# A four-layer image kernel on Trainium2: constant products in layer 2's last rows, hats sent in two lots, and the last group's norm and convolution at other steps

## What is computed

```python
x = x + _L0_conv_ref(_gn(x), ...)   # 1x1 convolutions and a mixture of radial bases
x = x + _L1_conv_ref(_gn(x), ...)   # state-space block
x = x + _L2_conv_ref(_gn(x), ...)   # attention, 8 heads over 256 pixels
x = x + _L3_conv_ref(_gn(x), ...)   # deformable 3x3 convolution
```

```python
offset = conv2d(x, off_w, off_b)
mask = jax.nn.sigmoid(conv2d(x, mask_w, mask_b))
samp = deform_sample(x, offset, mask)
out = jnp.einsum('bckhw,ock->bohw', samp, weight.reshape(O, C, K * K))
```

## Time and profile before

| | us |
|---|---|
| median of 3 runs (510.03 to 511.04) | 510.09 |
| the profiled execution's own time | 507.26 |
| its span | 505.4 |
| granted TensorE clock, mean over the span | 0.926 |
| TensorE busy (matmul) | 428.1 (85%) |
| VectorE busy | 346.9 (69%) |
| ScalarE busy | 280.1 (55%) |
| POOL busy | 133.4 (26%) |

### The profile page before, as it was taken

The page is one execution under the profiler, slowest core; times in us unless marked ns, Lnnn a source line. Parts: engine busy times, 40 slices in busy tenths (PEclk is TensorE's granted clock), DMA queues, the critical chain, the costliest instruction groups (busy, mean ns, idle before and its releaser), DMA issues.

```text
span 505.4 us, 9183 instructions
## 1 busy us (share of the span) xinstructions
PE 428.1 (85%) x3362; PEld 226.7 (45%) x3362; DVE 346.9 (69%) x672; ACT 280.1 (55%) x515; POOL 133.4 (26%) x171
## 2 busy tenths in 40 slices
PE   1525876899999998679998989998899999699997
PEld 0214755745555565513434434344355445255442
DVE  4538886423343556997998878978577768477785
ACT  1279974123135433605877778965486657376342
POOL 4330002100000001774544222232165245065000
PEclk9855998899999998756999999999799999999999
DMA  5400000630000000793320204407803923833500
GB/s 148 122 1 1 0 0 1 133 75 0 1 0 1 0 1 1 189 310 88 86 85 2 55 12 106 101 2 189 187 2 73 205 57 67 185 53 67 137 13 10
DMA packets 20170, 34.97 MB, mean 69 GB/s; under 512 B 4992, under 2 KB 16608, under 8 KB 18592
## 3 DMA queue, kind: packets, MB, share of 16 engines
q1 hardware_dynamic: 16880, 24.53, 20.6%
q0 software_dynamic: 1712, 7.01, 5.0%
q10 hardware_dynamic: 1536, 2.86, 2.2%
HBM read 16.78 MB, written 5.24 MB: 44 GB/s over the span
## 4 chain that ended last, share of the span: by engine, by line
PE 35%; DVE 8%; DMA 6%; POOL 5%; issue 3%; SPq 2%; ACT 2%; ACTq 1%; POOLq 0%; DVEq 0%
PE L_banks L1691 8%; PE L_banks L1593 6%; PE L_banks L1560 5%; PE L_banks L1667 4%; POOL L_parts L969 2%; PE L_banks L1631 2%; PE L_banks L1639 2%; DVE L_mx L1163 2%; DMA L_hats<-L_parts 2%; POOL L_rest L963 2%; DMA L_hat<-L_offsets 1%; SPq L1014 1%; ACTq L913 1%; PE L_banks L1573 1%; PE L_banks L1604 1%
## 5 line engine op out<-in xcount | busy, mean ns | idle before, releaser
L1163 DVE TENSOR_REDUCE L_mx<-L_banks 128x2 f32<-128x512 f32 x128 | 83.6, 687 | 14.2 <-PE L_banks L1560 13.3
L1285 DVE TENSOR_TENSOR L_s<-L_banks,L_cols 128x1024 f32<-128x1024 f32 x72 | 87.6, 1219 | 7.9 <-PE L_banks L1667 7.4
L1332 ACT ACTIVATE L_e<-L_banks 128x512 f32<-128x512 f32 x128 | 73.0, 596 | 28.0 <-PE L_banks L1573 26.1
L1691 PE MATMUL L_banks<-L_s,L_t_sb 128*64 128x256 f32 x576 | 80.7, 402 | 1.3 <-DVE L_s L1285 1.2
L1414 ACT ACTIVATE L_cols<-L_banks 128x512 f32<-128x512 f32 x72 | 42.9, 595 | 48.0 <-PE L_banks L1678 47.5
L1560 PE MATMUL L_banks<-stacks_k_st,stacks_q_st 64*128 64x256 bf16 x256 | 51.2, 300 | 6.5 <-DVE L_v_all L1150 4.2
L1691 PEld LDWEIGHTS L_banks<-L_s,L_t_sb 128*64 128x64 f32 x576 | 35.8, 139 | 35.7 <-DVE L_s L1285 19.7
L1573 PE MATMUL L_banks<-stacks_q_st,stacks_k_st 64*128 64x256 bf16 x256 | 47.0, 281 | 1.0 <-DMA stacks_q_st<-L_m_parts 1.0
L1667 PE MATMUL L_banks<-L_hats,L_sel 48*128 48x512 bf16 x144 | 44.6, 392 | 0.4 <-DVEq L1267 0.4
L1593 PE MATMUL L_banks<-L_e,L_v_x 128*32 128x256 f32 x512 | 41.1, 394 | 0.0
L1639 PE MATMUL L_banks<-all_w_all,L_xn 64*128 64x192 f32 x192 | 32.8, 337 | 2.8 <-ACT L_cols L1414 2.8
(11 more groups left out here) (264 smaller groups left out, 769.1 us busy)
## 6 DMA issues: line engine op xcount, KB each, us to landing
L_hats<-L_parts SPq DMA_DIRECT2D x28, 216.0 KB, 5.0
L_hat<-L_offsets SPq DMA_DIRECT2D x6, 576.0 KB, 6.9
L_stack<-L_xpad SPq DMA_DIRECT2D x12, 162.0 KB, 3.5
L_stack<-L_xpad SPq DMA_DIRECT2D x12, 153.0 KB, 4.0
L_mask<-L_masks SPq DMA_DIRECT2D x3, 576.0 KB, 10.8
stacks_q_st<-L_q_parts SPq DMA_DIRECT2D x12, 128.0 KB, 3.6
stacks_k_st<-L_k_parts ACTq DMA_DIRECT2D x12, 128.0 KB, 4.8
stacks_q_st<-L_q_parts POOLq DMA_DIRECT2D x12, 128.0 KB, 2.6
```

What stands on the lines that cost most here:

```text
L1163: dve.tensor_reduce(mx[:, n % 2, :, head], ring[:, place["largest", step] % 3].rearrange("p (q s) -> p q s", q=2), AX.X, ALU.max).then_inc ...
L1285: dve.tensor_tensor(s[:, q], row_ps[:, q], cols[:, t % 3:t % 3 + 1].broadcast_to([P, 2, 2 * N]), ALU.mult).then_inc(prod_ready, 1)
L1332: act.activation(e[:, k], ring[:, 3 + v % 3], ACT.Exp, scale=HD2 ** -0.5).then_inc(e_ready, 1)
L1691: mm = pe.matmul(acc[C * half:C * half + C, b, 0:N], t_sb[:, b, h, (KK * half + t) * C:(KK * half + t + 1) * C], s[:, q, h, half * N:(half ...
```

## The change

- In layer 2's rows 130 to 143 TensorE gets one constant product each, at the end of the row's work (in row 141 before the priming, so that rows 142 and 143 come behind it).
- In `next_chunk` the hats of b = 0 go in two lots: two thirds (taps 0 to 5) as soon as two thirds are split, the last third with its own semaphore, `first_hats_in[1]`. Each lot is four DMAs. TensorE waits for the second lot at tap 6, and ScalarE's first part of a later chunk waits for both.
- The last group's mean goes to step 2, its spread to 6, its convolution to 17, its mask's functions from 19. POOL does its variance behind the second mask product of chunk 1, its pad behind the third. SP sends the padded group ahead of chunk 1's hats.
- A constant `AHEAD` = 1 and the function `weighs` replace fixed conditions; for this value every condition, wait count and place is the one of before. The hunks with nothing but this are left out below, all but one.

```diff
--- before.py
+++ after.py
@@ -788,6 +788,7 @@
     CONV_AT = {67: 0, TAIL: 1, 128: 2}
     START = 8 * B + 13
     WEIGH_AT = {TAIL + 2 + 4 * k: k for k in range(6)}
+    AHEAD = 1
     LINES_AT = {60: 0, 64: 1}
     DIST_AT = {94: 0, 98: 1, 102: 2}
     OFFSETS_AT = {68: 0, TAIL + 1: 1, 130: 2}
@@ -814,15 +815,16 @@
     place = {user: n for n, user in enumerate(ring_users)}
 
 
-    MEAN_STEP, SPREAD_STEP, CONV_STEP = KK + 4, 2 * KK - 1, 2 * KK + 7
+    MEAN_STEP, SPREAD_STEP, CONV_STEP = 2, 6, 2 * KK - 1
     MASKS_STEP = CONV_STEP + 2
+    weighs = lambda n: AHEAD - 1 <= n < NP - 1
     col_users = [("cols", 0), ("cols", 1)]
     for n in range(NP):
         for t in range(KK):
             v = KK * n + t
             if v + 2 < KK * NP:
                 col_users.append(("cols", v + 2))
-            if t in WEIGHED and n < NP - 1:
+            if t in WEIGHED and weighs(n):
                 col_users.append(("t", 6 * n + 6 + WEIGHED.index(t)))
             if v in (MEAN_STEP, SPREAD_STEP, CONV_STEP):
                 col_users.append(({MEAN_STEP: "mean", SPREAD_STEP: "spread", CONV_STEP: "conv"}[v], NQ - 1))
@@ -1015,10 +1017,15 @@
 
                 def next_chunk(c):
 
-                    sp.wait_ge(parts3_ready, 3 * c + 3)
                     for b in range(2):
                         sp.wait_ge(prod_used, KK * (2 * (c - 1) + b) + 10)
-                        send_hats(c, b, hats_in[b])
+                        if b == 0:
+                            sp.wait_ge(parts3_ready, 3 * c + 2)
+                            send_hats(c, b, hats_in[0], slice(0, 2 * THIRD))
+                            sp.wait_ge(parts3_ready, 3 * c + 3)
+                            send_hats(c, b, first_hats_in[1], slice(2 * THIRD, TN))
+                        else:
+                            send_hats(c, b, hats_in[1])
                         if b == 0 and c < NQ - 1:
                             if c + 1 == NQ - 1:
                                 store_offsets(sp, c + 1, last_stored)
@@ -1035,9 +1042,8 @@
                     send_hats(0, 0, landed, slice(THIRD * j, THIRD * j + THIRD))
                 sp.wait_ge(s_ready, 8 * B)
                 send_hats(0, 1, hats_in[1])
-                next_chunk(1)
                 send_group(sp, NQ - 1)
-                for c in range(2, NQ):
+                for c in range(1, NQ):
                     next_chunk(c)
 
 
@@ -1126,9 +1132,10 @@
                     for hat_step, j in ((weigh_hat, 0), (weigh_hat, 1), (take_rest, 0), (weigh_hat, 2), (take_rest, 1), (take_last, 0),
                                         (take_rest, 2), (take_last, 1), (take_last, 2)):
                         hat_step(c, j)
-                    if c == 1:
-                        variance(NQ - 1)
-                        pad(NQ - 1)
+                        if c == 1 and (hat_step, j) == (weigh_hat, 1):
+                            variance(NQ - 1)
+                        if c == 1 and (hat_step, j) == (weigh_hat, 2):
+                            pad(NQ - 1)
 
             @block.vector
             def _(dve):
@@ -1227,7 +1234,7 @@
 
                     for half in range(2):
                         dve.wait_ge(first_ready, 2 * k + half + 1)
-                        dve.tensor_copy(t_sb[:, 0, k // 3, ds(half * KK * C + k % 3 * TW, TW)],
+                        dve.tensor_copy(t_sb[:, k // 6, k % 6 // 3, ds(half * KK * C + k % 3 * TW, TW)],
                                         ring[:, place["weigh", 2 * k + half] % 3, 0:TW]).then_inc(first_read, 1)
 
                 def take_first_image(b, w, k):
@@ -1396,8 +1402,8 @@
 
                     cut = slice(THIRD * j, THIRD * j + THIRD)
                     act.wait_ge(masked, 3 * c + j + 1)
-                    act.wait_ge(hats_in[0], 64 * c)
-                    act.wait_ge(hats_in[1], 64 * c)
+                    for landed in (*hats_in, first_hats_in[1]):
+                        act.wait_ge(landed, 64 * c)
                     act.activation(parts3[:, 0, cut], hat[:, c % 2, cut], ACT.Copy).then_inc(hi3_ready, 1)
 
                 def take_second(c, j):
@@ -1672,6 +1678,8 @@
                     c = col_at["cols", v]
                     if v in (0, 3):
                         pe.wait_ge(first_hats_in[v // 3], 64)
+                    if t == 6 and n and n % 2 == 0:
+                        pe.wait_ge(first_hats_in[1], 64 * (n // 2 + 1))
                     if v == 6 or (t == 0 and n):
                         pe.wait_ge(hats_in[n % 2], 64 * (n // 2 + 1))
                     col_free(c)
@@ -1726,9 +1734,11 @@
                         first_weights(WEIGH_AT[v])
                     if v == 8 * B + 1:
                         pe.wait_ge(e_ready, 8 * B)
+                    if v > 8 * B + 1:
+                        keep_clock(pe, avg2, ring[:, 5] if v <= START else acc[:, 1], 1)
                     if v == START:
                         pe.sem_inc(prod_used, 2)
-                        pe.wait_ge(first_read, first_done(6))
+                        pe.wait_ge(first_read, first_done(6 * AHEAD))
                         pe.wait_ge(off_ready, NQ - 1)
                         pe.wait_ge(sel_ready, 1)
                         spread_cols(0)
```

More of the change, by code:

```diff
@@ L916, in layers23 @@
         turn_of = lambda c: max(c, 1)
-        first_done = lambda w: w + 6
+        first_done = lambda w: min(w, 6 * AHEAD) + w
         norm_done = lambda g, step: len(NORM_STEPS) * g + step
@@ L1242, in _ @@
                 HATS_AT = {TAIL + n: step for n, step in enumerate(hat_steps)}
-                COPIES_AT = {TAIL + 3 + 4 * k: k for k in range(6)}
+                COPIES_AT = {v + 1: k for v, k in WEIGH_AT.items()}
                 LATE_LOG_AT = {TAIL + 7: 1, 137: 2}
@@ L1292, in _ @@
                 for n in range(NP):
-                    more = n < NP - 1
                     for t in range(KK):
-                        if t - 1 in WEIGHED and more:
+                        if t - 1 in WEIGHED and weighs(n):
                             k = WEIGHED.index(t - 1)
@@ L1479, in _ @@
                             take_cols(v + 2)
-                        if t in WEIGHED and more:
+                        if t in WEIGHED and weighs(n):
                             if t == WEIGHED[0]:
@@ L1502, in _ @@
                         if t == KK - 1 and n < NP - 2:
-                            if n:
+                            if n < AHEAD:
+                                act.wait_ge(first_ready, first_done(6 * n + 6))
+                            else:
                                 act.wait_ge(col_ready, col_at["t", 6 * n + 5] + 1)
-                            else:
-                                act.wait_ge(first_ready, first_done(6))
                             take_lines(n + 2)
@@ L1642, in first_weights @@
                 def first_weights(k):
-                    pe.wait_ge(xn3_ready, 1)
+                    pe.wait_ge(xn3_ready, k // 6 + 1)
                     at = [place["weigh", 2 * k + half] for half in range(2)]
-                    for half, mm in enumerate(weigh(0, k, [ring[:, at[half] % 3, 0:TW] for half in range(2)], lambda half: bank_free(at[half]))):
+                    for half, mm in enumerate(weigh(k // 6, k % 6, [ring[:, at[half] % 3, 0:TW] for half in range(2)], lambda half: bank_free(at[half]))):
                         mm.then_inc(first_ready, 1)
@@ L1686, in samples @@
                         pe.wait_ge(first_read, first_done(6 * n + 6))
-                        if n:
+                        if n >= AHEAD:
                             pe.wait_ge(col_read, col_at["t", 6 * n + 5] + 1)
```

## The result

| | before | after |
|---|---|---|
| median, us | 510.03 (5 runs, 508.90 to 511.04) | 504.36 (5 runs, 503.52 to 506.09) |
| profiled execution, us | 507.26 | 503.52 |
| its span, us | 505.4 | 501.7 |
| granted clock, mean | 0.926 | 0.938 |

The ratio is 0.9894, with a 95% interval of 0.9872 to 0.9917: 5.4 us faster (4.2 to 6.5). The forecast was 507.0 in 504.7 to 509.9: the direction held, the size was too small, and the measured median lies 0.3 us under the range. Compared again later, with more runs of both kernels, the changed kernel had 504.15 (8 runs) against 508.72 (31 runs), ratio 0.9921 (0.9894 to 0.9949): 4.0 us by the ratio, 4.6 by the medians.

The account below looks back on a forecast made before the run. TensorE was taken to bound the sampling, with gains only from stalls or low clock. Terms -2.4 (step 38), +0.6 (clock) and -1.3 (chunk 3's hats) sum to -3.1 us, from 510.09 to 507.0, range 504.7 to 509.9.

Parts of the forecast that it names:

- mean, spread: Last group's mean at step 2 and spread at step 6, both with a weight product: 0.7 us of TensorE each.
- step 38 against before: Step 38, waiting for chunk 3's positions behind SP's store: 2.4 us early, bounds 1 and 3.5.
- low clock, step 38 to 40: After step 38, a longer pause may lengthen TensorE's low clock: 0.6 us charged, bounds minus 0.5 and plus 1.6.
- wait for chunk 3's hats: Before step 52: the smaller, earlier first lot removes TensorE's wait, 1.3 us saved, bounds 0.8 and 1.3.
- Constant products: Rows 130 to 143: 14 products at 0.24 us; step 0 0.7 us late, clock held, net 1.5 us early at step 2.
- Lots, split, convolution, SP: Steps 16 to SP's store: chunk 2's split ends at 421.6, store at 425.2 instead of 427.38; lot 2 takes 2.6 back.
- the term after the store: From SP's store to chunk 3's landed positions: 12.35 us as before, then 2.60 to samples, less 0.2 for lighter landings.
- The rival that put 1.2 us on it: Better case: low clock not lengthened (0.6), landings before step 38 come 1.2 us sooner; 505.2 us, chance 0.13.
- the carried difference: Median of the runs stood 2.8 us above the profiled execution; the forecast kept that difference.
- The clock did not fall at the start: Rival at the start of sampling: clock falls all the same, step 38 gains nothing; 509.4 us, chance 0.15.
- the slower case: Rival in SP's queue: stores behind eight issues and late landings make step 38 2.5 us late; 511.9 us, chance 0.13.
- The rival by which the lots don't shrink the landing: Chunk 1's lot 1 lands at 393.7, as all did before; steps 16 and 38 1.4 later; 508.4 us, chance 0.06.

Follow-up runs that it names:

- products alone: Kernel before with only the 14 constant products added, profiled twice; ratio 1.0012 (0.9984 to 1.0039) to the kernel before.
- group alone: Kernel before with only the last group's norm, pad and convolution at the new steps; ratio 1.0034 (1.0010 to 1.0057) to the kernel before.
- changed with one lot: Changed kernel with all hats of the even pair sent at once; ratio 1.0052 (1.0023 to 1.0080) to the kernel before.
- stores between: Changed kernel with the last group's two stores on SP between the two lots of chunk 2's hats; 503.11 us (6 runs), ratio 0.9875 to the kernel before.
- before, again: The kernel before, unchanged, run once more for a second profile; 508.72 us, span 506.9.

## Why the prediction was right in mechanism and short in size

Counted from the mark (350.85 in the earlier trace rows), the steps of the text and what came:

| step of the prediction | predicted | measured |
|---|---|---|
| step 0 | 11.3 | 11.8 |
| clock from 355 to 366 | 1.00 | 1.00 |
| mean, spread | 0.7 each | 0.78, 0.79 |
| spread waits for POOL | no | no |
| chunk 1's split ends | 37.0 | 37.1 |
| step 16 | 42.1 | 42.2 |
| step 24 | 59.1 | 59.2 |
| chunk 2's split ends | 70.8 | 70.8 |
| SP's store of the offsets | 74.4 | 74.4, 74.3 |
| step 38 against before | -2.4 | -3.8, -4.1 |
| low clock, step 38 to 40 | +0.6 | +0.4, +1.4 |
| wait for chunk 3's hats | -1.3 | -1.3 |
| step 71 against before | -3.1 | -4.5, -4.0 |

**Constant products.** The clock held, as expected. Their price was 1.3 us at step 0 and not 0.7: the three products that I placed beside VectorE's addition stand ahead of the first column spread, and ScalarE's copy of that spread released the first sampling product. The chain has 0.86 us of products (L182) before the spread (L1686):

```profile
360.25 0.86 PE L_banks L182 x6
361.11 0.33 PE L_banks L1686
...
361.52 0.61 ACT L_cols L1420
...
362.22 1.24 DVE L_s L1292
```

So net 0.9 us early at step 2 (mean aside) and not 1.5. Chunk 1's lot made up for it: its last issue landed in 3.4 us where the prediction's 392.3 leaves a bit over 4, and nothing waited at step 16.

**Lots, split, convolution, SP.** All within 0.2 us, down to the store. The account was the right one: four more issues cost SP 2.3 us (5.05 for eight against 2.77 for four with the gap behind them; the prediction has 2.6), and the earlier split gives more than that. One sum there doesn't close: 386.16 and the 1.4 us of the pads make 387.6, and the text writes 387.8; measured is 387.9 on the same scale.

**The step that failed is the term after the store.** The prediction put "12.35 us from that issue to the landed positions" and took 0.2 off for lighter landings. The 12.35 has two parts. The stored masks landed in 3.99 us before, behind four issues of 216 KB sent just ahead; behind two lots, of which the first had left 5 us earlier and the second is 72 KB an issue, they landed in 1.81. All kernels with one lot (before, products alone, group alone, changed with one lot) have 3.9 to 4.0, those whose stores stand behind two lots 1.8. Three rows support that it is time in line, two of before, from TensorE's timeline and from the chain, and one of the kernel with the stores between the lots, from the DMA view (KB each, median us to landing):

```profile
431.56 0.39 PE L1678 MATMUL L_banks<-L_hats,L_sel 48*128 48x512 bf16 x1 [1.40 <-DMA L_hats<-L_parts]
428.02 3.99 DMA L_masks<-L_sig
L_masks<-L_sig SPq DMA_DIRECT2D x1, 128.0 KB, 2.4
```

The hats sent ahead of the masks released TensorE at 431.56, and the masks landed just behind them, at 432.01. Right behind four issues of 144 KB the masks took 2.4 us, between the two other values. So this part shrank by 2.2 us, not by 0.2. Of this the positions gave 1.0 back in the first profile (8.14 for 7.10) and 0.3 in the second (7.38). From there to step 38's samples it took 2.1 and 2.5 us instead of 2.60; in the first, TensorE's product ahead of them still ran at full clock (0.60 us, 1.01 before). Together that is 1.4 to 1.7 us beyond the term. My upper bound of 3.5 for this term was too low as well, and TensorE idled 3.67 and 2.90 us before step 38 where the prediction has about 5. The rival that put 1.2 us on it as "the landings on the way to step 38 come 1.2 us sooner, since less stands in line" has this half right, and had a chance of 0.13; its other half, a pause that doesn't lengthen the low clock, did not come (+0.4 and +1.4).

**The second failure is the carried difference.** "The median of the runs is 2.8 us above that execution; I carry the difference." The changed kernel's median is 0.8 above its own profiled execution. With 31 runs the kernel before has 508.72, 1.5 above. The 2.8 was a matter of which execution was profiled: executions differ ahead of the mark, and the difference was taken for a property of the kernel. Together: predicted gain 3.1; steps 1.4 more; the two carried differences 2.8 - 0.8 = 2.0 more; the mark 0.8 less: 5.7, the difference of the first medians. So of the 2.6 us that the forecast was short, 1.4 are the steps and 1.2 are how the executions fell. Against the larger set of runs, 4.0 to 4.6, the forecast of 3.1 is 1 to 1.5 short.

**The rivals.** The clock did not fall at the start. SP's queue did not turn into the slower case, since lot 2's issues were paid by the earlier split. The rival by which the lots don't shrink the landing falls: chunk 1's issues of 144 KB landed in 2.8 to 3.4 us, and the 216 KB ones at the same place before in 3.9 to 5.0. How much of that is bytes and how much time in line isn't separated, but the line has a part in it: of the four issues of 72 KB behind them the first landed in 3.0 us and the last in 2.1. What the changed kernel loses with one lot (6.7 us) says the same from the other side.

**What stays open.** Why the load of positions takes 10 us where the products stand alone, and why its two issues take longer in every kernel with the products that has them behind the hats and the stores; the expectations had no theory for it, and no further run was made for it. And what decides how long the clock stays low after step 38: where it fell there, steps 38 to 40 took 4.9 to 6.3 us.

## What to carry to other kernels

Before a transfer's time is copied from one profile into a forecast, ask what stood in the queue ahead of it: the landing of a small store can be mostly the landing of what was sent just before. When a pause late in the kernel is set by a chain through a DMA queue, follow that chain back to what its data need, and issue it as soon as they are there: here moving two stores and three loads ahead of hats that nobody needed yet gave more than the whole change. And a difference between one profiled execution and a median of three is no constant: find a mark ahead of the edit and count from it.

## What was not expected of the hardware

- A store of 128 KB landed in 4.0 us behind four issues of 216 KB, and in 1.8 us behind eight smaller ones of the same bytes begun 2.3 us earlier. Right behind four of 144 KB it was 2.4.
- Two issues of the same load took SP 1.19 us in the kernel before (both profiles) and 2.33 and 2.36 us with the products alone, and the load itself 10.30 and 9.71 us instead of 7.10. With the products and the other parts the issues took 1.73 to 1.93 us, but 1.19 and 1.23 where the stores had left earlier.
- Executions of one and the same program part differ by up to 4 us at a mark ahead of every edit (349.4 to 353.5), while the end, counted from that mark, repeats within 0.3 us (before), 0.6 (changed) and 1.4 (products alone).
- The length of the pause alone doesn't say whether the clock falls. At the wait for chunk 2's hats it stayed at 1.00 behind 1.40 us of idle in the first profile of before, and fell to 0.51 behind 1.33 in the second. Before step 38 it fell in every profile with 2.80 us of idle or more, and stayed at 1.00 behind 2.44 (stores between) and 1.44 (before, again).
